# Queries of the first cross attention turned by VectorE in 32x32 blocks and moved across partitions through DRAM, the query scale moved into the copy of the keys

## The reference

```
q = (layernorm(x) @ Wq + bq)  -> 16 heads of 128     k, v = (ctx @ Wk + bk), (ctx @ Wv + bv) -> 4 heads of 128
q = q * rsqrt(mean(q*q) + 1e-6) * qn_w               k = k * rsqrt(mean(k*k) + 1e-6) * kn_w
scores = q . k / sqrt(128) + mask      (each key head serves 4 query heads)
out = softmax(scores) @ v;  x = x + out @ Wo
```

## Time and profile before

| what | us |
|---|---|
| median of three runs | 3549.98 |
| the profiled execution | 3552.97 |
| its span (first to last instruction) | 3551.2 |
| TensorE matmuls busy | 3275.0 (92%) |
| VectorE busy | 2241.1 (63%) |
| ScalarE busy | 1868.7 (53%) |
| GpSimd busy | 83.2 (2%) |

### The profile page before, as it was taken

How to read it: one execution, slowest core, us unless ns; L and a number is a source line. 1 busy time by engine, 2 the same in 40 slices (tenths; PEclk the granted TensorE clock), 3 DMA queues, 4 the chain that set the end, 5 groups by cost and what they waited for, 6 DMA issues and landing times. The chain is left out here.

```text
span 3551.2 us, 74370 instructions
## 1 busy us (share of the span) xinstructions
PE 3275.0 (92%) x24736; PEld 2151.2 (61%) x24736; DVE 2241.1 (63%) x5883; ACT 1868.7 (53%) x5131; POOL 83.2 (2%) x134
## 2 busy tenths in 40 slices
PE   7999999999998998988888799999999999987799
PEld 4565666666653335556766466667666676656555
DVE  4556555555552226658887677777777777767832
ACT  4656656566553663336554555555555555534422
POOL 0000000000000000000000000000000000000000
PEclk8999999999998998999999899999999999998999
DMA  5333333334332002000000333333333333331000
GB/s 166 111 109 117 118 110 110 118 105 122 104 119 92 1 36 100 12 1 5 6 6 7 127 93 102 103 106 106 95 98 105 106 106 91 103 93 51 1 9 15
DMA packets 290410, 282.70 MB, mean 80 GB/s; under 512 B 20161, under 2 KB 235329, under 8 KB 288577
## 3 DMA queue, kind: packets, MB, share of 16 engines
q1 hardware_dynamic: 290240, 280.80, 26.0%
HBM read 206.02 MB, written 74.71 MB: 79 GB/s over the span
## 5 line engine op out<-in xcount | busy, mean ns | idle before, releaser
L480 PE MATMUL x_Kb<-x_cT,x_wk 128*128 128x257 f32 x3072 | 735.2, 386 | 41.0 <-ACT x_sq L732 20.6
L480 PEld LDWEIGHTS x_Kb<-x_cT,x_wk 128*128 128x128 f32 x3072 | 566.8, 190 | 237.9 <-issue 94.2
L508 PE MATMUL x_PC<-x_pT,x_cn 128*128 128x512 f32 x1024 | 475.9, 608 | 20.3 <-DMA x_pT<-x_probs_row 9.6
L746 ACT ACTIVATE x_pr<-x_pr,x_ntop 128x257 f32<-128x257 f32 x512 | 261.0, 510 | 369.7 <-DVE x_ntop L1018 190.0
L508 PEld LDWEIGHTS x_PC<-x_pT,x_cn 128*128 128x128 f32 x1024 | 185.5, 191 | 262.3 <-issue 251.4
L726 ACT ACTIVATE x_sq<-x_Kb 128x257 f32<-128x257 f32 x512 | 194.9, 381 | 164.5 <-DVE x_kT L994 157.7
L499 PE MATMUL x_Sb<-x_kT,x_qT 128*32 128x257 f32 (+1 forms) x4096 | 276.5, 384 | 4.9 <-DVE x_pr L1014 3.3
L994 DVE TENSOR_SCALAR x_kT<-x_Kb,x_vecs 128x257 f32<-128x257 f32 x512 | 240.1, 476 | 43.3 <-PE x_Kb L480 35.9
L752 ACT ACTIVATE x_pr<-x_pr,x_rps 128x257 f32<-128x257 f32 x512 | 241.1, 500 | 49.1 <-DVE x_rps L1024 45.2
L1034 DVE STREAM_TRANSPOSE x_turned<-x_pr 128x256 f32<-128x256 f32 x512 | 195.9, 420 | 60.5 <-ACT x_pr L752 42.9
L1048 DVE SCALAR_TENSOR_TENSOR x_pcT<-x_last,x_cT,x_PC 128x512 f32<-128x512 f32 x256 | 188.1, 737 | 43.6 <-PE x_PC L508 42.4
(11 more groups left out here) (316 smaller groups left out, 5790.5 us busy)
## 6 DMA issues: line engine op xcount, KB each, us to landing
x_probs_row<-x_turned SPq DMA_DIRECT2D x512, 128.0 KB, 2.3
x_pT<-x_probs_row SPq DMA_DIRECT2D x128, 512.0 KB, 3.8
x_cT<-in_ctxT SPq DMA_DIRECT2D x128, 257.0 KB, 4.3
x_cn<-in_ctx SPq DMA_DIRECT2D x128, 256.0 KB, 4.0
x_last<-x_last_row SPq DMA_DIRECT2D x128, 256.0 KB, 4.4
e_w<-in_e_w SPq DMA_DIRECT2D x3, 1152.0 KB, 7.7
c_staged_heads<-in_c_wqk SPq DMA_DIRECT2D x2, 1536.0 KB, 10.4
x_wq<-in_x_wq SPq DMA_DIRECT2D x1, 2048.0 KB, 8.0
```

The lines of the kernel that those rows point to most:

```text
L480: m = pe.matmul(key_bank(j)[:, 0:SE], wk[:, c, g * HD:(g + 1) * HD], cT[:, b, c, :], start=c == 0, stop=c == HC - 1)
L508: m = pe.matmul(PC[h][:, :], cn[:, b % 2, c, h * P:(h + 1) * P], pT[:, c, :], start=c == 0, stop=c == KC - 1)
L746: act.activation(pr[:, v, :], pr[:, v, :], ACT.Exp, bias=ntop[:, u:u + 1], scale=1.0 if L1 else -1.0, accum_out=ps[:, u:u + 1]).then_inc(e ...
```

## The change

In the first cross attention alone:

- TensorE's `transpose_query` (16 heads of each tile) and ScalarE's `copy_query` (four of each tile) are left out, with the waits that guarded their banks.
- VectorE gets `turn_query` right behind `norm_queries`: one block transpose of 128x512 for each group of four heads, into a new buffer `turned_q`. Before the first tile each of the four follows its norm.
- SyncE gets `store_queries` (four transfers of 32 partitions, 1 KB pieces) and `fetch_queries` (one transfer of 128 partitions), each for half of the heads, in the steps b = 0 and b = 2 of a tile; the load of the last row (`fetch_last`) is moved ahead of the context loads. `store_queries` waits for two turns, `fetch_queries` for its stores. The context loads of these steps stand between the two.
- GpSimd's copy waits for the two fetches in place of ScalarE's copies.
- ScalarE's key copy L730 multiplies by `qscale` (a column of 128 numbers) beside the bias; the bias is multiplied by it once (`bkq`).

```diff
+            def store_queries(t, z):
+                at = slice(z * 8 * S, (z + 1) * 8 * S)
+                sp.wait_ge(q_turned.sem, q_turned.now(t, 2 * (z + 1)))
+                for b in range(BT):
+                    sp.dma_start(queries_row[:, :, b, at].rearrange("m e n -> e m n"),
+                                 turned_q[S * b:S * (b + 1), :, at]).then_inc(q_stored.sem, 16)
+            def fetch_queries(t, z):
+                at = slice(z * 8 * S, (z + 1) * 8 * S)
+                sp.wait_ge(qT_ready.sem, qT_ready.before(t, BT))
+                sp.wait_ge(q_stored.sem, q_stored.now(t, z + 1))
+                sp.dma_start(qTn[:].rearrange("p b h q -> p b (h q)")[:, :, at],
+                             queries_row.rearrange("m e b n -> (m e) b n")[:, :, at]).then_inc(q_back.sem, 16)
...
                     fetch_probs(i, b)
+                    if not L1:
+                        fetch_last(i, b, nxt)
+                        if b in (0, 2) and nxt:
+                            store_queries(i + 1, b // 2)
...
-                    fetch_last(i, b, nxt)
+                    if L1:
+                        fetch_last(i, b, nxt)
+                    elif b in (0, 2) and nxt:
+                        fetch_queries(i + 1, b // 2)
...
+            if not L1:
+                for z in range(2):
+                    store_queries(0, z)
+                    fetch_queries(0, z)
             tile(0, True, True)
...
-                if s == 3 and nxt:
-                    if L1:
-                        pe.wait_ge(v_read.sem, v_read.now(i, 2))
+                if s == 3 and nxt and L1:
+                    pe.wait_ge(v_read.sem, v_read.now(i, 2))
                     transpose_query(i + 1, 2)
...
-                act.activation(kT[:, g, :], key_bank(j)[:, 0:SE], ACT.Identity, bias=bkv[:, 0, g:g + 1]
-                               ).then_inc(k_raw.sem, 1)
+                act.activation(kT[:, g, :], key_bank(j)[:, 0:SE], ACT.Identity, scale=qscale[:],
+                               bias=bkq[:, g:g + 1]).then_inc(k_raw.sem, 1)
...
-                    if s == 3 and nxt and not L1:
-                        copy_query(i + 1, 2)
-                        copy_query(i + 1, 3)
...
-                pool.wait_ge(qt_copied.sem, qt_copied.now(t, 4))
+                if L1:
+                    pool.wait_ge(qt_copied.sem, qt_copied.now(t, 4))
+                else:
+                    pool.wait_ge(q_back.sem, q_back.now(t, 2))
...
+            def turn_query(t, k):
+                dve.wait_ge(q_back.sem, q_back.before(t, 2))
+                dve.wait_ge(qn_done.sem, qn_done.now(t, k + 1))
+                dve.transpose(turned_q[:, :, k * 4 * S:(k + 1) * 4 * S].rearrange("p m (h q) -> p h m q", h=4),
+                              qn[:, 4 * k:4 * k + 4, :].rearrange("p h (m e) -> p h m e", m=4)
+                              ).then_inc(q_turned.sem, 1)
...
                 if s == 3 and nxt and not L1:
                     norm_queries(i + 1, 2)
                     norm_queries(i + 1, 3)
+                    turn_query(i + 1, 2)
+                    turn_query(i + 1, 3)
                 if cur:
                     shift_scores(i, s, 0)
...
                 if s == OUT_SLOT and nxt:
                     norm_queries(i + 1, 0)
                     norm_queries(i + 1, 1)
+                    if not L1:
+                        turn_query(i + 1, 0)
+                        turn_query(i + 1, 1)
```

More of the change, by code:

```diff
@@ L163, in cross_attention @@
             bq = sb("bq", [P, NH * HD])
+            bkq = sb("bkq", [P, G])
+            turned_q = sb("turned_q", [P, 4, NH * S])
+            queries_row = nc.dram_tensor(n + "queries_row", [4, S, BT, NH * S], F32, kind="Internal").ap()
             bkv = sb("bkv", [P, 2, G])
@@ L559, in first_piece @@
                         project_out(i - 1, range(0, NH // 2))
-                    if nxt:
-                        if prev and not L1:
-                            pe.wait_ge(v_read.sem, v_read.now(i - 1, 4))
+                    if nxt and L1:
                         transpose_query(i + 1, 0)
-                if s == 3 and nxt:
-                    if L1:
-                        pe.wait_ge(v_read.sem, v_read.now(i, 2))
+                if s == 3 and nxt and L1:
+                    pe.wait_ge(v_read.sem, v_read.now(i, 2))
                     transpose_query(i + 1, 2)
@@ L581, in second_piece @@
                         project_out(i - 1, range(NH // 2, NH))
-                    if nxt:
+                    if nxt and L1:
                         pe.wait_ge(qt_copied.sem, qt_copied.now(i + 1, 1))
                         transpose_query(i + 1, 1)
-                if s == 3 and nxt:
-                    pe.wait_ge(v_read.sem, v_read.now(i, 1 if L1 else 2))
+                if s == 3 and nxt and L1:
+                    pe.wait_ge(v_read.sem, v_read.now(i, 1))
                     transpose_query(i + 1, 3)
@@ L660, in _ @@
                 project_query(0, k)
[L661 to L667, removed]
+            pe.wait_ge(q_in.sem, q_in.now(0, 4))
+            if L1:
+                for k in range(4):
+                    if k in (1, 3):
+                        pe.wait_ge(qt_copied.sem, qt_copied.now(0, k // 2 + 1))
+                    transpose_query(0, k)
+                pe.wait_ge(qt_copied.sem, qt_copied.now(0, 4))
             pe.wait_ge(ready, 1)
@@ L712, in copy_query @@
                 dst = qTn[:, :, 4 * k:4 * k + 4, :].rearrange("p b h q -> p h b q")
[L713 to L716, removed]
+                act.activation(dst, src, ACT.Identity, scale=qscale[:], bias=qbias[:]).then_inc(qt_copied.sem, 1)
             def key(t, b, g):
@@ L759, in first_piece @@
                     square_query(i + 1, 2)
-                if s == OUT_SLOT and nxt:
+                if s == OUT_SLOT and nxt and L1:
                     copy_query(i + 1, 0)
@@ L850, in _ @@
             act.wait_ge(ready, 1)
-            for k in range(4):
-                copy_query(0, k)
+            if L1:
+                for k in range(4):
+                    copy_query(0, k)
             rsqrt_tokens(1)
@@ L891, in _ @@
                 s.prime(dve)
+            if not L1:
+                q_turned.prime(dve)
             if L1:
@@ L927, in _ @@
                 then(dve.scalar_tensor_tensor(qscale[:], nw[:, 0:1], SCALE, nw[:, 1:2], ALU.mult, ALU.mult))
+                then(dve.tensor_scalar(bkq[:], bkv[:, 0, :], qscale[:], None, ALU.mult))
                 then(dve.tensor_scalar(mask[:], mask[:], -1.0, None, ALU.mult))
@@ L973, in copy_queries @@
                 dve.wait_ge(q_done.sem, q_done.now(t, k + 1))
-                dve.wait_ge(qt_done.sem, qt_done.before(t, k + 1))
+                if L1:
+                    dve.wait_ge(qt_done.sem, qt_done.before(t, k + 1))
+                else:
+                    dve.wait_ge(q_turned.sem, q_turned.before(t, k + 1))
                 if L1:
@@ L1286, in _ @@
                 norm_queries(0, k)
+                if not L1:
+                    turn_query(0, k)
             if not L1:
```

14 lines of the change are left out of this document (12 added, 2 removed).

## The result

| kernel | median us (runs) | ratio to before, 95% interval |
|---|---|---|
| before, runs of the same session | 3553.44 (8) | |
| after | 3567.51 (8) | 1.0035 [1.0026, 1.0044] |

The change costs about 14 us. The forecast of 3564 was made against a median of 3549.98, so it meant +14. The profiled execution of after took 3563.82 us (span 3562.0), 10.85 more than that of before.

What follows compares the result with a forecast made beforehand. TensorE was taken to bound the first cross attention (busy 975.1 of 1006 us). Fifteen tiles at +0.42 us (+6.3) and the prologue's +7.5 gave +13.8, forecast 3564 us; own range 3556 to 3582, 8 in 10: 3545 to 3586.

Steps and rivals of the forecast that it cites:

- the main step: In slot 3, turns ahead of VectorE's score step delay it; TensorE's removed transposes only become waiting; +1.10 us.
- Slot 1: TensorE loses eight transposes, VectorE's two turns stay hidden by a wait; -0.95 us a tile, bounds 0.86 and 1.20.
- Keys: ScalarE's key copy slows from 475 to about 570 ns; 0.09 us in slots 0, 1 and 2, 0.27 a tile.
- Slot 3: Two VectorE turns, 1.35 us, move the score step from 607.95 to 609.30; +1.10 us, bounds +0.93 and +1.64.
- the unfilled slot: Last tile's slot without query work: 8.29 us from score step to key square, taken for the changed chain.
- The tile in sum: Each of 15 tiles making queries: -0.95 + 1.10 + 0.27 = +0.42 us, +6.3 in all.
- First scores: Before the first tile, stores queue behind weight loads; scores start at 41.6 instead of 36.38, +5.2 us.
- the restart's slow clock: Before the first tile, TensorE restarts at the 1.2 GHz level after waiting; 2.3 us charged.
- SyncE's round trip: Queries through DRAM in middle tiles, ready about 617.5 for scores at 622.1; 3.6 us to spare, no cost.
- Rival 1: TensorE's relief counts in full, slot 3 absorbing the turns; -1.93 us a tile, 3529 us, chance 0.12.
- Rival 2: Losses in slot 3 and the prologue are small; -0.25 us a tile, 3550 us, chance 0.20.
- Rival 3: The DRAM round trip decides, each tile waiting for GpSimd; 48 us more, 3612 us, chance 0.09.

Runs made afterwards that it cites:

- scale_only: Kernel before with the query scale moved from ScalarE's query copy into its key copy, transposes staying on TensorE; 3562.82 us, ratio 1.0026.
- filler: Kernel after plus 12 unread identity transposes on TensorE where it stands, ahead of the third scores; 3568.11 us, ratio 1.0045.
- turn_late: Kernel after with the last two turns of a tile moved behind both score steps; 3552.04 us, ratio 1.0001.
- combined: Kernel after with late turns, earlier semaphore releases, both halves stored before fetching, and query loads ahead of context loads; 3547.03 and 3547.71 us.
- before_padded: Kernel before with 56 useless semaphore increments added to VectorE's list ahead of its first wait; 3544.18 us, ratio 0.9971.

## Why the prediction was right, and where only the sum was

The sign, the range and the main step (slot 3 turns from a gain into a wait) held. That the number came out near is luck: the changed part lost 21.6 us where 13.8 were forecast, and a part that the forecast left out gave 8 back.

- Slot 1: -0.95 forecast, -0.93 measured.
- Keys: 0.09 in each of three slots forecast, 0.09 and 0.11 measured in slots 0 and 2 (15.39 to 15.48, 15.41 to 15.52), nothing that shows in slot 1; 0.27 a tile in scale_only.
- Slot 3: pair 1.35, measured 1.30; score step 3.3 behind the sums, measured 3.14; +1.10 forecast. Where the clock holds (157.83 to 173.63), the slot is 15.80 against 14.55, +1.25. Where it falls, 16.51. The 0.15 over the forecast is in the chain behind the step: from the step's start to the end of the key square it takes 8.67 us (160.97 to 169.64), where I took the 8.29 of the unfilled slot and 0.10. In before it was 8.64, so ScalarE's two query copies were not on this chain, and leaving them out gained nothing.
- **The term that failed in the tile:** I counted the 2 us in which TensorE waits as an idle time only, and charged a restart's slower clock before the first tile but not here. It is +0.3 a tile, some 4.6 us over 15 tiles; filler gave 5.3 back at the end of the first layer. The Trainium skill (TensorE: Matmul & The Clock Gate, Why this matters for your kernels) warns of idle gaps between bursts of matmuls; the gap that cost a clock here is shorter than those it warns of, so by its rule alone the term would have stayed out, and the measurement decides.
- The tile in sum: +0.42 forecast, +0.86 measured in each of 13, 11.2 us. The start up to and with the first tile took +8.3 (7.9 forecast, 7.5 and a tile's 0.42), the last tile that makes queries and what follows it +2.1 (0.42 forecast).
- Inside the start two errors cancelled as well. First scores came +7.3 for +5.2. The 2.3 for the restart's slow clock did not come on top: from the first scores to the end of the tile it was +1.0, hardly over a tile's 0.86, since before has its slow work at another place.
- SyncE's round trip: 1.86 us of issues and 3.8 to land were forecast; the fetch goes out at 626.53 and GpSimd begins at 631.67, 5.1 later, at a transfer share of 0.51 (0.38 before). Scores come at 636.48, so about 4 us are to spare (3.6 forecast). Turn_late shows where the spare time ends.
- **The term that was missing altogether:** -8 us in code that the change doesn't touch. Nothing in the parts of the change could give it. The sign was there to be read in before: stands with the releaser "issue" and 107 instruction packets. I had not looked at that part.
- Rival 1 (full relief, 3529): the tile got longer. Yet a part of it is seen in combined: with the turns off the chain a tile gains 0.7 us (1.93 in the rival). Rival 2 (3550) failed on slot 3. Rival 3 did not decide in after, only in turn_late.
- The figures of 390 and 311 ns in the prediction (the Trainium skill, VectorE: DVE Perf Modes, The three transpose paths) are for bf16, and this kernel is f32; here the eight transposes of slot 3 took 1.32 us, and a turn of 128x512 took 687 ns.

With the stands out of both, after compares with before_padded: 1.0035 and 0.9971 of before, so that the change itself costs some 23 us, and the combined version (3547.0 and 3547.7) is below the kernel before but not below before_padded. In the traces its first layer ends 3 to 7 us later than in before (1096.06 and 1099.86 against 1092.78 and 1093.37), so what it gains on before is the last part. The change in its best form found here is thus at best about level with leaving it out. A padded version of combined was not run; its last part (1574.4 and 1578.1) has no more stands to lose.

## What to carry to other kernels

Work taken off the busiest engine pays only in slots where that engine never waits; where it was filler, it turns into a wait, and if what replaces it stands ahead of the step that ends the wait, the loss is larger than the gain, with a lower clock on top. Put the new work behind that step, then look at what its own users now wait for. Before a difference of under half a per cent is put down to a change, compare stages that it doesn't touch: instructions added to an engine's list can move a later loop, and a padded copy of the old kernel shows what that alone is worth.

## What the runs showed of the hardware

- A stand of 2.17 us in a slot of some 16 us was enough for a granted clock of 0.69 in the 5.5 us behind it, in one tile of three; stands of 0.70 to 0.97 us were not. Behind a stand of the same length the clock held in another tile of three (the weighing took 3.70 us).
- VectorE can stand 25.7 us in a stage with the releaser "issue", depending on where in its list the loop lies (107 instruction packets against 46).
- VectorE turns 128x512 f32 in blocks in 687 ns. GpSimd multiplies the same size by a column in 1571 ns and copies it in 617.
- A column operand more on ScalarE (+89 ns) reached TensorE through the PSUM banks: 45 more waits of 0.15 to 0.2 us, though ScalarE is busy for only 57% (after) to 61% (scale_only) of the stage.
